# A six-stage decoder on one core: smaller normalisation steps with an operand in PSUM, scans, early row statistics, a third buffer of down weights, and a result stored by tiles

## The reference, cut to what matters

```python
x = x + attn0(layernorm(x))     # causal attention, 16 heads of 32
x = x + memory(layernorm(x))    # softmax readout of a 1024-row context, with a mask
x = x + moe0(layernorm(x))      # 16 experts, groups, top 6, SiLU gate*up, plus 2 shared halves
x = x + attn1(layernorm(x))     # RMS norm on top, rotary, 32 heads in 8 groups
x = x + linear(layernorm(x))    # attention with ReLU features
x = x + moe1(layernorm(x))      # 8 experts, softmax router, top 2, SiLU, plus 1 shared
```

## Time and profile before

| what | us |
|---|---|
| median of 3 runs | 2240.31 (2235.72 to 2246.98) |
| the profiled execution, own time | 2244.25 |
| its span, first to last instruction | 2242.6 |
| PE busy | 1892.7 (84% of the span) |
| DVE busy | 1136.9 (51%) |
| POOL busy | 963.4 (43%) |
| ACT busy | 789.2 (35%) |

### The profile page before, as it was taken

How to read it: one execution, slowest core, us unless ns; L and a number is a source line. 1 busy time by engine, 2 the same in 40 slices (tenths; PEclk the granted TensorE clock), 3 DMA queues, 4 the chain that set the end, 5 groups by cost and what they waited for, 6 DMA issues and landing times. The chain is left out here.

```text
span 2242.6 us, 30740 instructions
## 1 busy us (share of the span) xinstructions
PE 1892.7 (84%) x10524; PEld 1628.3 (73%) x10524; DVE 1136.9 (51%) x2349; ACT 789.2 (35%) x2043; POOL 963.4 (43%) x922
## 2 busy tenths in 40 slices
PE   4898958958799898699548999999997699896894
PEld 3676746747689797698536888888776588785784
DVE  4555675456233232234656666666664646446343
ACT  2555543221122121121036556555553323212231
POOL 2333332165682749721745545445352100005683
PEclk8999989989899999899869999999999799798997
DMA  2443531033653445421523333233320110002464
GB/s 80 132 119 121 183 118 38 1 117 142 219 192 119 152 146 189 158 88 53 170 71 93 94 80 82 67 90 80 81 67 26 64 55 1 20 1 91 175 221 150
DMA packets 102515, 232.32 MB, mean 104 GB/s; under 512 B 18640, under 2 KB 18896, under 8 KB 99296
## 3 DMA queue, kind: packets, MB, share of 16 engines
q1 hardware_dynamic: 82624, 144.89, 21.5%
q0 software_dynamic: 19744, 85.47, 11.1%
HBM read 126.23 MB, written 57.93 MB: 82 GB/s over the span
## 5 line engine op out<-in xcount | busy, mean ns | idle before, releaser
L558 POOL TENSOR_SCALAR a_E<-a_E,a_inv 128x128 f32<-128x128 f32 (+3 forms) x384 | 218.7, 587 | 280.3 <-DVE a_inv L670 280.3
L128 PE MATMUL bank<-f_UH,f_XH 128*128 x596 | 205.7, 345 | 45.8 <-POOL f_UL L140 40.5
L665 DVE TENSOR_REDUCE a_top<-bank 128x1 f32<-128x512 f32 (+3 forms) x384 | 164.4, 484 | 86.6 <-PE bank L808 84.3
L590 ACT ACTIVATE a_E<-bank,a_top 128x512 f32<-128x512 f32 (+3 forms) x384 | 198.7, 552 | 6.8 <-DVE a_top L665 6.8
L128 PE MATMUL bank<-f_UH,f_XL 128*128 x596 | 197.6, 332 | 0.0
L128 PE MATMUL bank<-f_UL,f_XH 128*128 x596 | 197.4, 331 | 0.0
L581 ACT ACTIVATE a_PHL<-bank 128x512 fp32r<-128x512 f32 (+1 forms) x288 | 130.8, 528 | 184.0 <-PE bank L824 183.9
L128 PE MATMUL bank<-a_PHL,a_VH 128*128 128x512 f32 (+3 forms) x768 | 181.1, 324 | 0.3 <-DVE a_QL L140 0.3
L140 DVE TENSOR_TENSOR a_PHL<-bank,a_PHL 128x512 fp32r<-128x512 f32 (+1 forms) x288 | 154.6, 591 | 29.6 <-ACT a_PHL L581 29.0
L1483 DVE TENSOR_TENSOR f_gate<-bank,f_gate 128x352 f32<-128x352 f32 x79 | 41.4, 524 | 239.5 <-PE bank L128 239.5
L128 PEld LDWEIGHTS bank<-f_UH,f_XH 128*128 128x128 f32 x596 | 117.0, 196 | 48.5 <-issue 48.5
(11 more groups left out here) (394 smaller groups left out, 5180.5 us busy)
## 6 DMA issues: line engine op xcount, KB each, us to landing
f_uraw<-f_up POOLq DMA_DIRECT2D x18, 1408.0 KB, 6.5
f_xb<-table SPq DMA_DIRECT2D x86, 256.0 KB, 2.9
table<-f_ob SPq DMA_DIRECT2D x86, 256.0 KB, 2.0
table<-a_zeros SPq DMA_DIRECT2D x31, 512.0 KB, 3.9
f_draw<-f_down POOLq DMA_DIRECT2D x27, 512.0 KB, 4.3
a_g<-a_f SPq DMA_DIRECT2D x160, 64.0 KB, 2.0
a_raw<-a_qkv SPq DMA_DIRECT2D x36, 256.0 KB, 3.1
f_uraw<-f_up POOLq DMA_DIRECT2D x9, 704.0 KB, 4.6
```

The costliest lines, as they stand in the source:

```text
L128: m = pe.matmul(out, a, b, start=first and i == 0 and j == 0, stop=last and i == n - 1 and j == 2, skip_group_check=not check)
L558: e.tensor_scalar(self.E[sl][:, a], self.E[sl][:, a], self.inv[:, sl, i:i + 1], 0.0, ALU.mult, ALU.add).then_inc(*self.s_nrm.up(N, m - 1, i))
L590: x = e.activation(self.E[sl][:, self.E_AT[i]:self.E_AT[i] + w], bank[:, off:off + w], ACT.Exp, bias=self.top[:, sl, i:i + 1], accum_out=s ...
L665: e.tensor_reduce(self.top[:, sl, i:i + 1], bank[:, off:off + P * (i + 1)], AX.X, ALU.max, negate=True).then_inc(*self.s_mx.up(N, m, i))
```

## The change

- Norm: the root on ACT goes. `_inverse_root` on DVE starts from a bit pattern (shift, subtract from a constant) and makes three Newton steps of three instructions. Most small steps now have one operand or the output in PSUM (`small(n)`, a corner of bank 6). `bn_stats` of a tile is issued right behind the last write of that tile (`row_stats`), in the stage before.
- Routing: small tiles move to PSUM banks 0 and 7 (`banked`); the two prefix sums by doubling become one `tensor_tensor_scan` each (`_sums`); `_some` takes 8 and 10 steps in place of 5 and 9 (the second mixture keeps 3 and 7); the product for `share` moves behind the indices.
- `DB` = 3. `_down(2)` goes ahead of the scatters and loses its wait, and `_up(w)`, `_down(w)` of one expert follow one another. `XH`, `XL`, `HH`, `HL` and `gate` have one buffer in place of two, and shared steps ahead of the routed ones use PSUM bank 6 alone.
- The result is stored by eight DMAs, each behind the last add of its tile.

```diff
     def _inverse_root(self, var, eps, to):
-        e.wait_ge(*self.s_root.after(self.name, r))
-        e.reciprocal(i, self.root[:, :]).then_inc(*d.up())
...
+        v, u, i = self.var[:, :], self.u[:, :], self.small(0)
+        e.tensor_scalar(v, var, eps, None, ALU.add).then_inc(*d.up())
+        e.wait_ge(*d.now())
+        e.tensor_scalar(i.bitcast(I32), v.bitcast(I32), 1, None, ALU.logical_shift_right).then_inc(*d.up())
+        e.wait_ge(*d.now())
+        e.tensor_scalar(i.bitcast(I32), i.bitcast(I32), -1.0, float(0x5F3759DF), ALU.mult, ALU.add).then_inc(*d.up())
+        e.wait_ge(*d.now())
+        for n in range(3):
+            e.scalar_tensor_tensor(out=u, in0=i, scalar=-0.5, in1=v, op0=ALU.mult, op1=ALU.mult).then_inc(*d.up())
+            e.wait_ge(*d.now())
+            e.scalar_tensor_tensor(out=u, in0=u, scalar=1.0, in1=i, op0=ALU.mult, op1=ALU.mult).then_inc(*d.up())
+            e.wait_ge(*d.now())
+            e.scalar_tensor_tensor(out=i if n < 2 else to, in0=u, scalar=1.5, in1=i, op0=ALU.add, op1=ALU.mult).then_inc(
+                *d.up())
+            e.wait_ge(*d.now())
...
     def act(self, meanwhile=lambda: None, then=lambda i: None):
-        for r in range(1 if self.rms is None else 2):
-            e.wait_ge(*self.s_var.after(self.name, r))
-            e.activation(self.root[:, :], self.var[:, :], ACT.Sqrt).then_inc(*self.s_root.up(self.name, r))
...
                 e.tensor_tensor(X[:, g, :], bank[:, :], X[:, g, :], ALU.add).then_inc(*self.s_x.up(N, j, g))
+                if j == self.STEPS - 1:
+                    e.wait_ge(*self.s_x.after(N, j, g))
+                    self.k.row_stats(g)
...
-    XB, OB, UB, DB = 3, 2, 3, 2
+    XB, OB, UB, DB = 3, 2, 3, 3
...
+    def out_bank(self, n):
+        return 6 if n < self.first else 6 + n % 2
...
-        self._up(1)
-        self._down(1)
-        self._up(2)
+        for w in (1, 2):
+            self._up(w)
+            self._down(w)
         for j in range(self.top):
             e.wait_ge(*self.s_idx.after(N, j))
-            if j == 2:
-                self._down(2)
...
         self._up(3)
+        self._down(3)
...
-            self._down(w - 1)
             if w < W:
                 self._up(w)
+                self._down(w)
...
     def _down(self, w):
-        if w == self.DB:
-            e.wait_ge(*self.s_out.after(N, NT - 1))
...
-            if n >= 2:
-                e.wait_ge(*self.s_out.after(N, n - 2))
+            if n >= 1:
+                e.wait_ge(*self.s_out.after(N, n - 1))
             for ps, cs, src in self._transposed():
-                m = e.activation(self.HH[ps, n % 2, cs, :], src, ACT.Copy)
+                m = e.activation(self.HH[ps, cs, :], src, ACT.Copy)
...
             if n < NT:
-                self._some(routing, 5 if self.gated else 3)
+                self._some(routing, 8 if self.gated else 3)
...
-                self._some(routing, 200 if n == NT - 1 else 9 if self.gated else 7)
+                self._some(routing, 200 if n == NT - 1 else 10 if self.gated else 7)
...
+    def _sums(self, to, x):
+        self.k.dve.tensor_tensor_scan(out=to.rearrange("p t r -> p (t r)"), data0=self.go.rearrange("p t r -> p (t r)"),
+                                      data1=x.rearrange("p t r -> p (t r)"), initial=0.0, op0=ALU.mult,
+                                      op1=ALU.add).then_inc(*self.k.d.up())
...
-        emptied[7] = self.s_prob.after(N) if self.bias is not None else self.s_shifted.after(N)
+        emptied[7] = self.s_place.after(N)
...
-        k.sp.wait_ge(*entry)
-        k.sp.dma_start(rows(t["out"]), k.X[:, :, :]).then_inc(*s_end.up())
+        for i in range(NT):
+            k.sp.wait_ge(*stage.done(i))
+            k.sp.dma_start(rows(t["out"])[:, i:i + 1, :], k.X[:, i:i + 1, :]).then_inc(*s_end.up())
```

More of the change, by code:

```diff
@@ L194, in _centre, with small, dve @@
                         ALU.subtract, ALU.mult).then_inc(*self.s_y.up(self.name, i))
[L196 to L201, removed]
+    def small(self, n):
+        return self.k.bank[6][:, n * NT:(n + 1) * NT]
+    def dve(self):
+        e, d = self.k.dve, self.k.d
@@ L652, in dve @@
             e.wait_ge(*entry)
-        self.norm.dve(loaded)
+        for i in range(NT if loaded is not None else 0):
+            if i % 2 == 0:
+                e.wait_ge(*loaded[i // 2])
+            self.k.row_stats(i)
+        self.norm.dve()
         if self.rotary is not None:
@@ L1543, in _add, with _ranks @@
         self.x_last[i] = self.s_x.after(N, j, i)
[L1545 to L1549 removed]
+        if j == self.top - 1 and self.bias is not None:
+            e.wait_ge(*self.x_last[i])
+            self.k.row_stats(i)
+    def _ranks(self, v, same, before, ge, top):
+        e, d, n = self.k.dve, self.k.d, v.shape[-1]
         e.memset(before, 0.0).then_inc(*d.up())
@@ L1607, in _largest @@
         yield
[L1608 to L1609 removed]
+        self._sums(nth, equal)
         yield
[L1611 removed]
         e.wait_ge(*d.now())
@@ L1619, in _largest @@
         e.wait_ge(*d.now())
-        e.tensor_tensor(above, above, equal, ALU.add).then_inc(*d.up())
+        e.tensor_tensor(above, above, both, ALU.add).then_inc(*d.up())
         yield
@@ L1629, in _route @@
         each = lambda a: a.rearrange("p (t a) -> p t a", a=1).broadcast_to([P, NT, R])
-        two, chosen = (yield from self._upto("upto", R)), early("chosen", [NT, R])
+        self.go, chosen = self.banked(7, P, [NT, R]), early("chosen", [NT, R])
+        e.wait_ge(*self.s_logits.after(N))
+        e.memset(self.go, 1.0).then_inc(*d.up())
+        yield
+        e.wait_ge(*d.now())
+        e.memset(self.go[:, :, 0:1], 0.0).then_inc(*d.up())
+        yield
         kept = self.taken["early"]
@@ L1721, in _route @@
         yield
-        one, spot = [late(f"one{i}", [NT, R]) for i in range(2)], late("spot", [self.top, NT])
+        ones = late("one", [2 * NT, R])
+        one, spot = [ones[:, 0:NT, :], ones[:, NT:, :]], late("spot", [self.top, NT])
         e.wait_ge(*self.s_place.after(N))
@@ L1735, in _route @@
             yield
-        yield from self._tables(end)
+        yield from self._tables(end, ones, late("count", [self.NR]))
+        e.tensor_tensor(self.turns(share), self.in_turn(sc), self.turns(mine), ALU.mult).then_inc(*d.up())
+        yield
         e.wait_ge(*d.now())
```

243 lines of the change are left out of this document (120 added, 123 removed).

## The result

The changed kernel takes 2181.39 us (median of 4 runs, 2174.97 to 2185.81), the kernel before beside it 2240.60: a ratio of 0.9732, 95% interval 0.9697 to 0.9767. It is faster by 59 us; the sum had 75.2 and the forecast time was 2167. The measured time lies in the range of 2150 to 2194, at the upper edge of the first case (2153 to 2182). The profiled execution took 2185.81, with a span of 2184.6, so by the profiles 58.0 us of span are gone.

What follows compares the result with a forecast made beforehand. PE was taken as the bound, with POOL's order of work twice on the path in the first mixture. 22.8 + 27.5 + 14.7 + 4.8 + 0.9 + 4.5 = 75.2 us gave a forecast of 2167 us, range 2150 to 2194.

Steps and rivals of the forecast that it cites:

- the first case: The forecast as worked out: 2167 us, between 2153 and 2182; chance 0.62.
- Scatters and routing: First mixture: down conversion ahead of the scatters gives 11.0 us, a sooner first index 12.4; gain taken as 22.8.
- Order for UL: Routed experts: up conversion of w before down of w-1 shortens PE's UL waits, 27.5 us; second mixture 4.8.
- Routing's own cost: First mixture's shared tiles: DVE's earlier count wait delays HL, about 2.5 us of PE's time; second mixture 1.5 lost.
- Norm entries: Stage starts: bn_stats of 4.84 us leave, the new root's chain takes 3.8 for 2.3; together 14.7 us gained.
- Second attention: 4.0, bounds 2 and 5: Second attention's entry: 4.84 us of bn_stats and two roots, less two ACT trips with a table load; 4.0 gained.
- Memory: 4.5, bounds 1 and 7.5: Memory's entry: less waiting for the root and held steps, limited by ACT's context copies and later adds; 4.5 us gained.
- Store: End of kernel: 7.4 us after the last add become about 2.9, the landing of 256 KB; 4.5 gained (3 to 5.4).
- the case of the late index: Rival: first mixture's index comes no sooner because DVE is blocked; 11 in place of 22.8, 2179 us; chance 0.14.
- DL waits: Rival: routed experts' UL waits turn into DL waits, the 27.5 shrink to 4, 2190 us; chance 0.12.
- One buffer each: Rival: single buffers serialise ACT and DVE with PE, 1.3 us a tile over 86 routed tiles, 2279 us; chance 0.04.
- PSUM steps: Rival: some 150 small DVE steps are each 0.03 us dearer, costing 5 us, 2172 us; chance 0.06.

Runs made afterwards that it cites:

- the second profile: The changed kernel run once more without any edit, against the kernel before: ratio 0.9717, 2179.6 us.
- buffers and conversion alone: The kernel before with three down buffers, single XH, HH and gate and POOL's new order, but old routing, norms and store: 0.9836 of the kernel before, 2206.1 us.
- old_order: The changed kernel with POOL's earlier order behind the scatters, down conversion of w-1 ahead of up conversion w, three down buffers kept: 0.9859 of the kernel before, 2210.1 us.
- norm_in_bank: The changed kernel with the norm's last single-source mean and variance steps reading PSUM too: 0.9671 of the kernel before, 2170.0 us.
- one_store: The changed kernel with one store of all eight tiles behind the last add in place of eight: 0.9738 of the kernel before, 2185.8 us.

## Why the prediction was right, and where it was off

**Scatters and routing (22.8).** Right: 23.15 us at the sixth row transpose, of which 0.7 came from the stages ahead. In the second profile these stages cost 3.0 us (the last memory add is at 456.3, before at 453.3), and 22.7 are left for this term. Its parts hold as well: 11.07 for buffers and conversion alone against 11.0. One thing was added up in the wrong place: 5.6 of these 11.0 are the conversion, and the rest the wait for a down buffer, which goes with the third buffer wherever the conversion stands.

**Order for UL (27.5, and 4.8 in the second mixture).** Right: 26.1 and 29.6 us from the sixth to the last row transpose in the two profiles, and old_order takes back 28 to 32 in all. Waits of 2.2 to 2.5 us were left, as forecast, and none for DL. The pair of one-tile experts gave 5.5 in place of 7.3 (2.16 + 9.64 left of 9.57 + 7.69), which is why the waits for UL are 16.4 (14.8 in the second profile) and not under 14. In the second mixture old_order takes 169.1 us from entry to last row transpose where the changed kernel took 164.5 and 166.2.

**Routing's own cost.** PE's wait for HL was 2.33 us at 506.82 and 1.50 in the second mixture: 2.5 and 1.5 were forecast.

**Norm entries (14.7).** Here the forecast is off, by three of its six numbers. The first attention's 0.3 came out as 0.6 us later at the first centring: the new chain is 1.5 longer there too, and of 2.1 us of holds 1.3 are left, where the sum let them go. "Second attention: 4.0, bounds 2 and 5" measured 0.5 and 1.3, outside the bounds. The step that failed is that a hold was priced only where the trace of before had one. Single-source steps were known to be held, and the clearings were in the trace; that a chain which starts 4.84 us sooner runs into them was not looked at. norm_in_bank shows it: without the held steps the entry is 4.0 sooner. "Memory: 4.5, bounds 1 and 7.5": the first reduction came 1.0 us sooner and, in the second profile, 1.0 later. Counted from the start of the first attention's last four adds, so without what that stage lost (0.8 and 1.8), it is 1.8 and 0.8. The sum counted ACT's copies of the context and the adds' delay, and still took the middle, where what decides, the load that follows the last add, pointed to the lower end; and it put at nothing the 1.7 us that the lower granted clock takes back. Linear and second mixture came as forecast: from last add to entry 3.0 and 3.3 us less. The first mixture's entry came 2.9 nearer to the last add; the forecast has this in the scatters' term, as "the 3 us by which its work begins sooner".

**Store (4.5).** 5.3 at the end, less 1.4 for the gathers: 3.9 and, with the adds as they fell, 3.6.

**What was not in the sum.** The linear stage took 275.2 us from entry to last add in both profiles with the old code, and 278.4 and 278.3 changed; that is why its next line in the table has 0.1 and 0.2 and not 2.9. It is TensorE's clock. In the windows view (busy us of PE, PEld, DVE, ACT, POOL, then the granted clock, DMA share and GB/s) of the whole stage and of two stretches of 10 us, at 170 and at 260 us behind the entry, changed kernel:

```profile
1700.15:1979.26 279.11, 256.51 (x1340) 221.74 (x1340) 152.67 (x255) 81.95 (x134) 18.77 (x12) 0.87 0.08 26
1870.15:1880.15 10.00, 8.51 (x24) 6.41 (x24) 3.37 (x3) 2.19 (x4) 2.96 (x2) 0.71 0.37 105
1960.15:1970.15 10.00, 10.00 (x53) 8.82 (x53) 5.49 (x14) 1.20 (x2) 0.00 (x0) 0.77 0.00 0
```

and one_store, whose code is the same up to the last store:

```profile
1698.85:1974.73 275.88, 252.41 (x1340) 218.62 (x1340) 152.58 (x255) 82.11 (x134) 18.77 (x12) 0.88 0.08 26
1868.85:1878.85 10.00, 7.09 (x24) 5.35 (x24) 3.76 (x3) 2.19 (x4) 2.95 (x2) 0.84 0.34 105
1958.85:1968.85 10.00, 10.00 (x58) 8.71 (x57) 5.68 (x13) 1.20 (x2) 0.00 (x0) 0.92 0.00 0
```

The same 1340 matmuls keep PE busy for 256.5 us in one and 252.4 in the other, while its idle time is 22.6 and 23.5: the 3 us are matmuls that ran at the lower level, 1.2 GHz, and not waits. Over all thirteen profiles the stage took 273.6 to 278.4; of the eleven with the new norms seven lie at 277.3 or above. In all seven of these PE stood 5.2 to 5.9 us for `lin_KL`, some 184 us behind the entry, and in the six short ones 6.4 to 6.6. This wait marks the two cases; which of the two brings the other about is not shown. Whether the change makes the long case more likely, or chance did, stays open. The second attention (590.4 to 598.0 over the thirteen; 592.8 and 593.6 with the old norms) differs between executions of one program, whatever the change does to it: it put 4.4 us against the first profile and 2.4 in favour of the second. Of the 6.8 us between these two, 2.3 are PE's busy time and 3.4 its waits for the loads of `a_QL` (10.7 and 7.3).

**The rivals.** None came. By the time alone the case of the late index (2179) would fit better than the 2167; the index at 508.7 (510 forecast, 522.5 before) and the sixth row transpose rule it out. DL waits: none. One buffer each: the pitch of the routed tiles stays at 6.69 us. PSUM steps: 166 ns. Of the signs named in advance two failed: waits for UL under 14 us, and a first centred tile 3 to 6 us after each entry. From the last add to the start of centring it was 4.6 us in the memory stage, 6.8 and 6.3 in the mixtures, 12.1 in the second attention and 16.1 in the linear stage.

## What to carry to other kernels

When work is moved earlier on one engine, read what the other engines do in the time it moves into: a chain of small steps that starts sooner can land beside POOL work that holds it, and the gain is gone. Where such a hold is seen, give every step of the chain a source in PSUM, the last few too; and where one entry of a stage waits for a load, ask what the load itself waits for before pricing a faster chain beside it.

## What the hardware showed that was not expected

- A DVE step of 128x8 with one float source in SBUF was held by a POOL instruction that only writes, a MEMSET: 3.69 and 4.56 us. With the source in PSUM and the result in SBUF it took 0.15.
- Where both may run undisturbed, the same step takes 166 ns with its operand in SBUF or in PSUM.
- Eight stores of 256 KB beside the last gathers raised the median from issue to landing of a gather from 3.8 to 4.6 us, made the last add 1.4 us later, and ended 2.1 us behind the last add where one store of 2048 KB took 7.4.
- Code that is the same had the linear stage at 275 or at 278 us, with 4.1 us more of busy PE time for the same matmuls, and the second attention between 590 and 598. A term of 3 us in such a stage can be seen only by marks from the timeline, not in the median.
- PE started the memory stage's products 2.7 us sooner after a start in pieces, and lost 1.7 of it at a granted clock of 0.62 in place of 1.00.
